# A three-phase layer on one core: output bias added in the setup, a rounding moved from ScalarE to VectorE, two phases rolled into loops

## The reference, cut to what matters

```python
x = x + cross_attention(layernorm(x), ctx)        # x: 16 batches x 128 x 512, ctx: 16 x 2048 x 512, 16 heads
x = x + mamba_block(layernorm(x))                 # selective scan, inner width 1024, 16 states, then an MLP
x = x + experts(layernorm(x))                     # shared and expert projection, top-2 gate

def cross_attention(q_in, c):
    q, k, v = q_in @ wq.T + bq, c @ wk.T + bk, c @ wv.T + bv
    return softmax(q @ k.T * scale) @ v @ wo.T + bo

def mamba(Z):                                     # inside the block, followed by rmsnorm(y + Z)
    x, z = split(Z @ in_proj.T)
    x = silu(causal_conv4(x))
    dt, B, C = split(x @ x_proj.T)
    dt = softplus(dt @ dt_proj + dt_b)
    h[t] = exp(dt * A) * h[t-1] + dt * B * x      # per channel (1024) and state (16)
    y = sum(h * C) + x * D
    return (y * silu(z)) @ out_proj.T
```

## Time and profile before

| | |
|---|---|
| median of 3 executions | 4108.15 us (4107.05 to 4108.25) |
| the profiled execution, own time | 4108.25 us |
| its span in the profile | 4106.5 us |
| TensorE busy, granted clock | 94% of the span, 0.984 |
| VectorE busy | 70% |
| ScalarE, GpSimd busy | 42%, 28% |

### The profile page before, as it was taken

The page is one execution under the profiler, slowest core; times in us unless marked ns, Lnnn a source line. Parts: engine busy times, 40 slices in busy tenths (PEclk is TensorE's granted clock), DMA queues, the critical chain, the costliest instruction groups (busy, mean ns, idle before and its releaser), DMA issues. The chain is left out here.

```text
span 4106.5 us, 83418 instructions
## 1 busy us (share of the span) xinstructions
PE 3861.9 (94%) x34816; PEld 2797.0 (68%) x34816; DVE 2865.6 (70%) x3017; ACT 1740.1 (42%) x3466; POOL 1153.5 (28%) x547
## 2 busy tenths in 40 slices
PE   8999999999999999999999977898999888699998
PEld 6777877777777777777777764454445543388876
DVE  5667657766766766776676657999999999754433
ACT  2324424433432442443343236776677667322221
POOL 1111011011111101111111105766787678410000
PEclk9999999999999999999999989999999999899999
DMA  4110110011011011001101021220211111220000
GB/s 151 38 42 28 38 52 30 28 50 43 28 38 42 28 40 50 30 28 50 43 28 38 29 99 57 57 57 14 59 57 57 31 41 47 68 79 26 31 21 16
DMA packets 96789, 183.73 MB, mean 45 GB/s; under 512 B 8337, under 2 KB 12817, under 8 KB 96434
## 3 DMA queue, kind: packets, MB, share of 16 engines
q1 hardware_dynamic: 96434, 178.27, 13.7%
HBM read 152.82 MB, written 25.43 MB: 43 GB/s over the span
## 5 line engine op out<-in xcount | busy, mean ns | idle before, releaser
L238 POOL TENSOR_TENSOR c_lo<-c_raw,c_hi 128x2048 fp32r<-128x2048 f32 x64 | 294.9, 4607 | 1973.2 <-DVE c_hi L341 1973.2
L953 POOL TENSOR_TENSOR b_drive<-b_dt_u,b_bc 128x1024 f32<-128x1024 f32 x256 | 599.9, 2357 | 294.1 <-PE b_y L1380 253.7
L429 DVE TENSOR_TENSOR prob_sums<-prob_sums,probs 128x1024 f32<-128x1024 f32 x480 | 566.7, 1222 | 113.8 <-ACT probs L313 113.8
L402 DVE TENSOR_REDUCE max_parts<-scores 128x2 f32<-128x1024 f32 x512 | 601.9, 1218 | 40.5 <-PE scores L563 40.5
L313 ACT ACTIVATE probs<-scores 128x512 f32<-128x512 f32 x1024 | 528.9, 604 | 213.9 <-PE scores L594 213.9
L1380 PE MATMUL b_y<-b_drive,b_ident 128*128 128x512 f32 x1024 | 502.8, 619 | 117.2 <-DVE b_drive L1245 115.8
L1234 DVE TENSOR_TENSOR_SCAN b_decay<-b_decay,b_drive 128x1024 f32<-128x1024 f32 x256 | 585.5, 2287 | 24.0 <-ACT b_decay L1102 23.4
L394 DVE SCALAR_TENSOR_TENSOR k_lo<-scores,bk_sb,k_hi 128x512 fp32r<-128x512 f32 x256 | 192.4, 751 | 564.3 <-ACT k_hi L298 564.3
L298 ACT ACTIVATE k_hi<-scores,bk_sb 128x512 fp32r<-128x512 f32 x256 | 176.3, 689 | 603.2 <-PE scores L515 603.2
L1380 PEld LDWEIGHTS b_y<-b_drive,b_ident 128*128 128x128 f32 x1024 | 187.4, 193 | 354.8 <-DVE b_drive L1245 197.0
L1102 ACT ACTIVATE b_decay<-b_dt,b_a 128x254 f32<-128x254 f32 x1024 | 425.0, 461 | 0.4
(11 more groups left out here) (220 smaller groups left out, 6277.0 us busy)
## 6 DMA issues: line engine op xcount, KB each, us to landing
c_raw<-in_ctx SPq DMA_DIRECT2D x64, 1024.0 KB, 5.2
b_bc<-bc_scratch SPq DMA_DIRECT2D x128, 256.0 KB, 4.4
q_scratch<-v_sb SPq DMA_DIRECT2D x4, 1024.0 KB, 4.3
q_raw<-q_scratch SPq DMA_DIRECT2D x16, 256.0 KB, 5.2
q_raw<-in_x SPq DMA_DIRECT2D x16, 256.0 KB, 3.2
x_scratch<-q_raw SPq DMA_DIRECT2D x16, 256.0 KB, 5.8
attn_scratch<-attn_out_sb SPq DMA_DIRECT2D x16, 256.0 KB, 2.0
b_attn<-attn_scratch SPq DMA_DIRECT2D x8, 512.0 KB, 4.1
```

Of the source, the lines that this page charges most:

```text
L238: pool.tensor_tensor(c_lo[:, slot], c_raw[:], c_hi[:, slot].bitcast(F32), ALU.subtract).then_inc(c_lo_ready, 1)
L402: dve.tensor_reduce(max_parts[:, g, 2 * pair:2 * pair + 2, s], max_banks[:, 2 * pair:2 * pair + 2, :], AX.X, ALU.max).then_inc(max_taken, 1)
L429: dve.tensor_tensor(part, part, probs[:, u % 4], ALU.add).then_inc(summed, 1)
L953: pool.tensor_tensor(drive[:, m % 4], dt_u[:, 2 * p:2 * p + 2, :].unsqueeze(1).to_broadcast([P, SG, 2, T]), bc[:, g, 0].unsqueeze(2).to_br ...
```

## The change

1. Phase A: `x + bo` is made in the setup, on the four 128 x 2048 tiles `x_sb` after they have been normalised, and stored from there; the reload, the addition and the store in each batch are gone, and the next batch's queries are loaded as soon as the query buffer has been split. The load of `bo` goes ahead in SyncE's queue, into `out_sb`. GpSimd's order in the setup is written anew.
2. Phase B: ScalarE's `round_sum` (two operations) becomes one `tensor_scalar` on VectorE, behind units 25 and 27 (`DVE_M`).
3. Phase B: the table of positions is changed; waits on `sum_ready` in `layernorm` and `turn` are dropped.
4. Phases B and C: the six middle steps run in a `Fori` of three iterations with two steps each.

```diff
+        bo_rows = out_sb[:].rearrange("p g t -> p (g t)")
...
             load_x(1)
+            sp.dma_start(bo_rows, bo.partition_broadcast(P)).then_inc(bo_loaded, 16)
...
-            sp.dma_start(bo_rows[:], bo.partition_broadcast(P)).then_inc(bo_loaded, 16)
-            sp.wait_ge(xn_ready, 1)
+            def store_x(i):
+                sp.wait_ge(bo_added, i + 1)
+                sp.dma_start(x_out_v[i], x_sb[i]).then_inc(x_stored, 16)
+
+            store_x(0)
+            sp.wait_ge(x_stored, 16)
             load_x(3)
             store_queries(0)
             sp.wait_ge(q_stored, 16)
             sp.dma_start(q_raw[:], q_dram[0]).then_inc(q_loaded, 16)
-            sp.wait_ge(xn_ready, 2)
+            store_x(1)
+            sp.wait_ge(x_stored, 2 * 16)
             load(0, 0)
             for i in range(1, q_steps):
                 store_queries(i)
+            store_x(2)
+            store_x(3)
             sp.wait_ge(q_stored, q_steps * 16)
+            sp.wait_ge(x_stored, q_steps * 16)
...
-                    if s == 0:
+                    if s == 0 and not last:
                         sp.wait_ge(q_split, (i + 1) * 2)
-                        sp.dma_start(x_tile, x[i]).then_inc(x_tile_loaded, 16)
+                        sp.dma_start(q_raw[:], q_dram[i + 1]).then_inc(q_loaded, 16)
...
-                    if s == 2:
-                        sp.wait_ge(bo_added, i + 1)
-                        sp.dma_start(x_dram[i], x_tile).then_inc(x_stored, 16)
-                if not last:
-                    sp.wait_ge(x_stored, (i + 1) * 16)
-                    sp.dma_start(q_raw[:], q_dram[i + 1]).then_inc(q_loaded, 16)
...
             def add_bo(i):
-                pool.wait_ge(x_tile_loaded, (i + 1) * 16)
-                pool.tensor_tensor(x_tile, x_tile, bo_rows[:], ALU.add).then_inc(bo_added, 1)
+                pool.wait_ge(xn_ready, i + 1)
+                pool.tensor_tensor(x_sb[i], x_sb[i], bo_rows.unsqueeze(1).to_broadcast([P, group, width]),
+                                   ALU.add).then_inc(bo_added, 1)
+            make_rstd(0)
+            make_rstd(1)
             pool.wait_ge(bo_loaded, 16)
             add_bo(0)
-            for s in range(2, blocks):
+            make_rstd(2)
+            add_bo(1)
+            make_rstd(3)
+            low_part(0, 0)
+            add_bo(2)
+            add_bo(3)
+            for s in range(1, blocks):
                 low_part(s, s % 2)
...
                 if g == 0:
+                    dve.wait_ge(bo_added, q_steps)
...
-    PE_HEADS, PE_OUT_LAST, PE_TURN, PE_IN_X, PE_X, PE_DT = (0, 2), 4, 7, (9, 10, 11, 13), 19, (21, 23)
-    PE_IN_Z, PE_OUT = (14, 15, 16, 17, 22, 24, 26, 28), (27, 29, 31)
-    POOL_DT_U1, POOL_DT_H1, POOL_DT_U2, POOL_DT_U3, POOL_RSTD, POOL_OUT = 0, 3, 6, 8, 6, 11
+    PE_HEADS, PE_OUT_LAST, PE_TURN, PE_IN_X, PE_X, PE_DT = (0, 3), 1, 7, (9, 10, 11, 13), 19, (21, 23)
+    PE_IN_Z, PE_OUT = (14, 15, 16, 17, 20, 22, 24, 25), (27, 29, 31)
+    POOL_DT_U1, POOL_DT_H1, POOL_DT_U2, POOL_DT_U3, POOL_RSTD, POOL_OUT = 0, 2, 4, 5, 7, 9
...
-    ACT_LOG1, ACT_SQUARES, ACT_XN, ACT_XN_T, ACT_SCALE, ACT_TAP, ACT_U = 1, 9, 8, 10, 14, (12, 13, 15, 17), 18
-    ACT_Z, ACT_DBC, ACT_ABS, ACT_EXP, ACT_LOG0, ACT_GATE = (19, 20, 27, 31), 22, (24, 26), (25, 27), 28, 4
+    ACT_LOG1, ACT_SQUARES, ACT_XN, ACT_XN_T, ACT_SCALE, ACT_TAP, ACT_U = 1, 7, 8, 10, 11, (12, 13, 15, 17), 18
+    ACT_Z, ACT_DBC, ACT_ABS, ACT_EXP, ACT_LOG0, ACT_GATE = (19, 20, 25, 29), 22, (24, 26), (25, 27), 28, 4
...
-    DVE_SUM, DVE_X1, DVE_CONV = 6, (2, 4), (12, 13, 14, 16)
+    DVE_SUM, DVE_X1, DVE_CONV = 4, (3, 5), (12, 13, 14, 16)
+    DVE_M = (25, 27)
...
-            for i in range(1, steps - 1):
-                body(i, i % 2, False, False)
+            with eng.Fori(0, (steps - 2) // 2) as k:
+                body(k * 2 + 1, 1, False, False)
+                body(k * 2 + 2, 0, False, False)
...
-            def round_sum(j, h):
-
-                act.wait_ge(exp_ready, j * 2 + h + 1)
-                act.activation(e_round[h], e_neg[h], ACT.Copy, bias=1.0).then_inc(one_added, 1)
-                act.wait_ge(one_added, j * 2 + h + 1)
-                act.activation(e_round[h], e_round[h], ACT.Copy, bias=-1.0).then_inc(rounded, 1)
...
+            def round_sum(j, h):
+
+                dve.wait_ge(exp_ready, j * 2 + h + 1)
+                dve.tensor_scalar(e_round[h], e_neg[h], 1.0, -1.0, ALU.add, ALU.add).then_inc(rounded, 1)
```

More of the change, by code:

```diff
@@ L139, in cross_attention @@
         q_stored = sem("q_stored")
-        bo_loaded, x_tile_loaded = sem("a_bo_loaded"), sem("a_x_tile_loaded")
-        bo_added, x_stored = sem("a_bo_added"), sem("a_x_stored")
+        bo_loaded, bo_added, x_stored = sem("q_bo_loaded"), sem("q_bo_added"), sem("q_x_stored")
         block = ctx.enter_context(nc.Block())
         ctx_v = ctx_t.rearrange("b (k p) s -> b p k s", p=P)
-        x_v = x.rearrange("(s b) t d -> s t b d", b=group)
+        x_v, x_out_v = (t.rearrange("(s b) t d -> s t b d", b=group) for t in (x, x_dram))
         q_v = q_dram.rearrange("(s b) p g t -> s p b g t", b=group)
@@ L221, in _ @@
             sp.wait_ge(attn_stored, 16 * (batches + 1))
-            sp.wait_ge(x_stored, 16 * batches)
         @block.gpsimd
@@ L247, in add_bo @@
             def add_bo(i):
-                pool.wait_ge(x_tile_loaded, (i + 1) * 16)
-                pool.tensor_tensor(x_tile, x_tile, bo_rows[:], ALU.add).then_inc(bo_added, 1)
-            for i in range(q_steps):
-                make_rstd(i)
-            low_part(0, 0)
-            low_part(1, 1)
+                pool.wait_ge(xn_ready, i + 1)
[3 more added lines that the diff above has]
+            make_rstd(1)
             pool.wait_ge(bo_loaded, 16)
             add_bo(0)
-            for s in range(2, blocks):
+            make_rstd(2)
[5 more added lines that the diff above has]
+            for s in range(1, blocks):
                 low_part(s, s % 2)
             with pool.Fori(1, batches) as i:
-                low_part(i * blocks, 0)
-                low_part(i * blocks + 1, 1)
-                add_bo(i)
-                for s in range(2, blocks):
+                for s in range(blocks):
                     low_part(i * blocks + s, s % 2)
@@ L997, in layernorm @@
                 act.wait_ge(shift_ready, j * 2 + 2)
-                if j >= 2:
-                    act.wait_ge(sum_ready, (j - 1) * group)
                 for b in range(group):
@@ L1082, in front @@
                 exp_of_abs(j, 0)
-                round_sum(j, 0)
                 take_t(j, par, 1)
                 exp_of_abs(j, 1)
-                round_sum(j, 1)
                 log(j, 0)
@@ L1132, in body @@
                         exp_of_abs(j, ACT_EXP.index(m))
-                        round_sum(j, ACT_EXP.index(m))
                     if m == ACT_LOG0:
@@ L1177, in convolve @@
                 ins.then_inc(x_taken, 1)
+            def round_sum(j, h):
+                dve.wait_ge(exp_ready, j * 2 + h + 1)
+                dve.tensor_scalar(e_round[h], e_neg[h], 1.0, -1.0, ALU.add, ALU.add).then_inc(rounded, 1)
             def rounding_error(j, h):
+                round_sum(j, h)
                 dve.wait_ge(rounded, j * 2 + h + 1)
@@ L1256, in body @@
                         convolve(j, 1 - par, DVE_CONV.index(m))
+                    if m in DVE_M:
+                        round_sum(j, DVE_M.index(m))
                 if not last:
@@ L1285, in turn @@
                 pe.wait_ge(xn_ready, j + 1)
-                if j >= 2:
-                    pe.wait_ge(sum_ready, (j - 1) * group)
                 for b in range(group):
```

3 lines of the change are left out of this document (removed).

## The result

The changed kernel takes 4135.4 us (median of four executions, 4135.3 to 4136.4), the kernel before in the same session 4108.2 (4107.1 to 4109.1): a ratio of 1.0067 with a 95% interval of 1.0051 to 1.0083. That is 27.2 us more; the forecast was 21.4 more (4130), with a range of its own of 4118 to 4143. The profiled execution has a span of 4135.9 us against 4106.5, 29.4 more. It was a somewhat long one: its own time was 4138.0 us, 2.6 over the median, while the profiled execution of the kernel before took 4108.25.

The account below looks back on a forecast made before the run. TensorE was taken to bound phases A and C, VectorE phase B. The terms 9.9 - 17.3 + 25.9 - 3.3 - 7.8 + 1 + 12 + 1 gave +21.4 us, so 4130 us, range 4118 to 4143.

Parts of the forecast that it names:

- Part 1, bias: Setup of phase A: GpSimd's additions hold two VectorE normalises, 4.6 us each, plus 0.7 for a load: +9.9 us.
- The +0.7 for the load of the second context block: Phase A: stores ahead of block (0,1)'s load delay VectorE's cast of it: +0.7 us, bounds 0 and 2.
- Part 2, ScalarE's relief: Phase B: without its rounding, ScalarE no longer makes the scans of units 28 and 29 wait: -17.3 us.
- VectorE's roundings: Phase B, behind units 25 and 27: new tensor_scalars, held by GpSimd's drives, cost 3.7 us a step: +25.9 us.
- GpSimd keeps the port pair: Rival, phase B: behind unit 27 VectorE's rounding waits one or two more GpSimd instructions; 4147 to 4155 us, chance 0.11.
- The front: Front of phase B: log 0 comes earlier without ScalarE's roundings ahead of it: -3.3 us, bounds -1 and -4.2.
- Heads: Phase B: VectorE adds heads at units 3 and 5, so waits of 0.75 and 3.27 us go: -7.8 us.
- `make_dt` ahead of drive 3: Phase B, GpSimd: drive 3 comes later, its scan no longer put off by an addition: +1 us in all.
- z at unit 20: Phase B, TensorE: a z projection behind unit 20 adds 1.73 us waiting for unit 23's sum each step: +12 us.
- Loops: Phases B and C: two back edges in each cost +1 us, bounds 0 and +6.
- The sign that I gave for a wrong prediction: Loops: the prediction is wrong if a back edge shows a gap of more than 1 us.
- The loop stalls: Rival: each back edge costs an instruction fetch and followers fall late, +6 to +11 us, 4135 to 4140; chance 0.08.

Follow-up runs that it names:

- e4: The changed kernel with GpSimd's addition of the bias to x(i) also waiting for the normalise of step i + 1: 4133.2 us.
- e11: The kernel before with only the bias added to x in the setup of phase A instead of in its loop: 4120.2 us.
- e8: e7 with the first half's rounding on VectorE ahead of unit 25's product, the second still on ScalarE: 4110.7 us.
- e2: The changed kernel with VectorE's rounding ahead of the product of units 25 and 26 instead of behind that of units 25 and 27: 4134.2 us.
- e5: The kernel before with only the rounding moved from ScalarE to VectorE, as in the change: 4116.3 us.
- e1: The changed kernel with phase B's steps written out again, its loop removed, phase C's loop kept: 4133.2 us.
- e7: The kernel before with the new positions, but z projections at their old places, ScalarE's rounding and no loop: 4110.8 us.
- e3: The changed kernel with TensorE's z projections of the third and fourth pair back behind units 22, 24, 26 and 28: 4129.8 us.
- e6: The kernel before with only the middle steps of phases B and C put in loops, as in the change: 4115.3 us.

## Why the prediction came out right, point by point

**Part 1, bias, +9.9.** Right in place, and in size partly by luck. Each of the two normalises was held by 4.2 us, forecast 4.6, together 8.5 instead of 9.2; in e4 the hold is gone when GpSimd is not beside it. The other 1.5 us were in no term: 0.5 are there ahead of the normalise of step 1 (24.18 against 23.67), 0.1 and 0.8 come with the turns at the lower clock, 0.2 behind the last normalise. That TensorE, kept waiting, is then slower was not thought of. The +0.7 for the load of the second context block came as well, but behind the first key product, and smaller. Time line of the changed kernel, VectorE:

```profile
97.30 1.23 DVE L344 CAST c_hi<-c_raw 128x2048 fp32r<-128x2048 f32 x1 [0.47 <-DMA c_raw<-in_ctx]
```

All seven kernels with the new setup have this wait, 0.4 to 0.6 us, and none of the others. e11 shows no gain in the loop, as forecast.

**Part 2, ScalarE's relief, -17.3.** Right: all waits at units 28 and 29 went. e8 shows that the first rounding alone does not bring it, which the prediction did not tell apart.

**VectorE's roundings, +25.9.** Right: 2.37 + 1.56 = 3.9 us a step, forecast 3.7 (its terms add up to 3.64, so 25.5 and not 25.9), 27.5 in all. The first was held 1.77 us (forecast 1.7), the second 1.0 (forecast 0.8). e2 shows that it is the company of GpSimd and nothing in the instruction: the same tensor_scalar at 0.68 us. "GpSimd keeps the port pair" did not happen: VectorE got in behind the one instruction that was under way. The Trainium skill ("SBUF — State Buffer", § Who interferes with whom) says that whoever issues first has the shared pair for the whole instruction and the other is blocked. The trace agrees both ways: where VectorE's rounding stood first GpSimd's next instruction took longer, 2.80 instead of 2.35 us in the changed kernel and in e2.

**The front, -3.3.** It measured 2.7: 55.9 us from VectorE's first instruction of phase B to the first scan, against 58.6, and 3.1 in e5 (55.5). The table doesn't show it in the changed kernel, because the loop of phase A took 2197.3 us from a place in its first batch to the same place in its last, against 2195.6, and the load above 0.5 more. With the same loop e1 took 2194.8 and e4 2198.1, so I count the 1.7 as spread and not as an effect.

**Heads, -7.8.** Right to 0.1 us in the trace (3.3 and 0.75 x 6).

**`make_dt` ahead of drive 3, +1 in all.** This step failed in size. I counted a single small delay where there is one in each step: 1.27 in five steps of the changed kernel (6.3 us), 1.80 in seven steps of e7 (12.6). The reason given, that the scan is "no longer put off by an addition", was exactly what uncovered it: in the kernel before the additions at unit 2 hid drive 3, and the same edit took them from there and put two instructions of GpSimd, 4.7 us, ahead of it.

**z at unit 20, +12.** The mechanism was right: 2.26 us at unit 24 in every step, forecast 2.3, and e3 gets 10.8 back. But in the changed kernel the waits at the end of a pair grew by 5.7 us in all, not 12: what VectorE lost elsewhere, at unit 3, in the roundings and behind back edges, let TensorE be ready at units 8 and 16, where waits of up to 1.5 us had been: 12.0 us in all became 5.6. This part was in no term, and which loss gave it is my reading; no run tests it.

**Loops, +1.** This step failed. The earlier trace rows are of TensorE in phase A, and I carried them over to another engine and another phase. The back edge costs VectorE 2.6 to 3.8 us each time in phase B: 6.5 by its waits in the changed kernel, 6.9 us scan to scan in e6, 4.0 in e1. Behind the last scan the six kernels with phase C's loop took 563.7 to 565.5 us and the eight without it 562.7 to 564.2, so there it costs about 1 us. That is between 5 and 8 us in all, at the end of the bounds of 0 to 6 and not near the 1 that was taken. The sign that I gave for a wrong prediction, a back edge with a gap of more than 1 us, did appear. For this term the rival *The loop stalls* was right, to which I had given 0.08, and the measured 4135.4 us lies in its 4135 to 4140.

Put together: 10.0 (setup) - 0.2 (to the first scan, by the table) + 27.5 - 17.3 (rounding) - 7.8 (heads) + 6.3 (drive 3) + 5.7 (pair ends) + 6.5 (back edges) - 1.4 (small scan waits of the first and last step that went) + 0.9 (behind the last scan) = 30.2, against 29.4 in the spans. The forecast was 6 to 8 us low: drive 3 and the loops were too small by 5 each and the roundings by 2, and the waits at the ends of pairs were 6 less than the z term said. So the place of most terms was right, but that the total came this near is in part luck, since a miss of 6 us one way stood against misses of 12 the other way.

## What to carry to other kernels

Look for what an instruction that you move is hiding: additions that stand ahead of a scan pay for themselves as long as the scan's inputs are not ready, and a position is worth something only together with the positions of the engines that feed it. A VectorE instruction that GpSimd can hold is cheap or dear by a few tenths of a microsecond of where it starts, so put it where GpSimd is still waiting for its own input, and check that its result doesn't release GpSimd onto the next one. Price a loop's back edge on the engine that bounds the phase, and when a wait's releaser is named, see when that releaser had ended before it is believed. Ask too what an engine that is kept waiting does next: here TensorE came back at half its clock.

## What the runs showed that was not expected

- A back edge of a loop costs 2.6 to 3.8 us on VectorE and makes ScalarE 0.75 to 3.5 us late in phase B, where its body is two steps of 32 units long; GpSimd showed no gap there, and TensorE in phase A 0.8 us in 14 batches. The trace puts VectorE's stall down to the engine that released it last; only once, in e2, did it name it "issue".
- Four tensor_scalars in a row that meet one GpSimd instruction are held once, until it ends (6.14 us instead of 1.92), not four times.
- A tensor_tensor of VectorE is held as well: beside GpSimd's last two additions in the setup the first `q_lo` of the changed kernel took 4.98 us instead of 0.69. It cost nothing, since it ended 16 us ahead of the first product with the queries.

```profile
68.42 4.98 DVE L392 TENSOR_TENSOR q_lo<-q_raw,q_hi 128x512 fp32r<-128x512 f32 x1
```

- A store of 1 MB issued 0.4 us behind a load of 1 MB was waited for 8.8 us instead of 4.6 to 5.0.
